# Turning the attention weights by 32x32 blocks and DMAs instead of matrix transposes, in a four-layer graph kernel

## The reference, cut to what matters

```python
Wh = jnp.einsum('bnf,fo->bno', h, W)
s1, s2 = Wh @ a1, Wh @ a2
e = s1[:, :, None] + s2[:, None, :]
e = jnp.where(e >= 0, e, ALPHA * e)
e = jnp.where(adj_matrix[None] == 0, -jnp.inf, e)
attention = jax.nn.softmax(e, axis=-1)
h_prime = jnp.einsum('bij,bjo->bio', attention, Wh)
```

## Time and profile before

| | |
|---|---|
| time, median of 3 runs | 634.5 us (633.63 to 634.8) |
| time of the profiled execution | 635.21 us |
| its span, first to last instruction | 633.4 us |
| mean granted clock of PE | 0.996 of full speed |
| slots 3 to 6, each | 57.5 us |
| slots 2 and 7 | 57.3 and 57.6 us |

### The profile page before, as it was taken

The page is one execution under the profiler, slowest core; times in us unless marked ns, Lnnn a source line. Parts: engine busy times, 40 slices in busy tenths (PEclk is TensorE's granted clock), DMA queues, the critical chain, the costliest instruction groups (busy, mean ns, idle before and its releaser), DMA issues.

```text
span 633.4 us, 9530 instructions
## 1 busy us (share of the span) xinstructions
PE 617.9 (98%) x2738; PEld 433.9 (68%) x2738; DVE 470.4 (74%) x1623; ACT 435.6 (69%) x1000; POOL 167.3 (26%) x228
## 2 busy tenths in 40 slices
PE   9999999999999999999999999999999999999994
PEld 6645556448975686578568757865885686577794
DVE  3999999877847658866887787688769867365656
ACT  3678786957847765784777678567857766546774
POOL 1465541005332003204403240340143032103201
PEclk9999999999999999999999999999999999999998
DMA  8334000000000000000000000000000000000000
GB/s 331 136 130 167 1 2 0 0 1 2 1 1 1 1 2 0 2 1 34 2 1 1 33 2 1 35 2 1 1 33 2 0 35 1 1 0 35 1 35 35
DMA packets 4372, 16.85 MB, mean 27 GB/s; under 512 B 480, under 2 KB 480, under 8 KB 4192
## 3 DMA queue, kind: packets, MB, share of 16 engines
q1 hardware_dynamic: 4320, 16.25, 6.7%
HBM read 12.05 MB, written 4.19 MB: 26 GB/s over the span
## 4 chain that ended last, share of the span: by engine, by line
PE 77%; DVE 3%; ACT 3%; issue 2%; POOL 1%; ACTq 0%; POOLq 0%; DVEq 0%
PE QQ L855 26%; PE QQ L867 15%; PE PA L838 4%; PE PA L810 4%; PE PB L829 2%; PE PB L820 2%; PE PB L691 2%; PE PA L691 2%; PE PA L791 2%; PE PB L791 2%; PE PA L644 1%; PE QQ L889 1%; PE PB L908 1%; PE PB L770 1%; PE PA L770 1%
## 5 line engine op out<-in xcount | busy, mean ns | idle before, releaser
L1231 ACT ACTIVATE raw<-QQ,BL 128x256 f32<-128x256 f32 (+2 forms) x279 | 150.1, 558 | 75.1 <-PE QQ L867 37.7
L855 PE MATMUL QQ<-HT,WT 128*128 128x256 f32 (+2 forms) x558 | 183.9, 474 | 1.1 <-ACT raw L1231 0.6
L450 POOL TENSOR_TENSOR RSD<-VAR,pw 128x4 f32<-128x4 f32 (+1 forms) x43 | 61.8, 1438 | 376.2 <-DVE VAR L1454 376.2
L855 PEld LDWEIGHTS QQ<-HT,WT 128*128 128x128 f32 x558 | 103.5, 190 | 59.3 <-issue 28.3
L867 PE MATMUL QQ<-HB,WT 128*128 128x256 f32 (+2 forms) x336 | 100.2, 441 | 0.4 <-DVE HB L1740 0.2
L867 PEld LDWEIGHTS QQ<-HB,WT 128*128 128x128 f32 x336 | 61.2, 190 | 29.3 <-issue 13.4
L1267 ACT ACTIVATE raw<-raw 128x256 f32<-128x256 f32 (+4 forms) x79 | 37.1, 470 | 25.9 <-DVE raw L1722 19.7
L1712 DVE SCALAR_TENSOR_TENSOR raw<-raw 128x256 f32<-128x256 f32 (+2 forms) x60 | 32.5, 542 | 20.2 <-ACT raw L1231 19.6
L1740 DVE SCALAR_TENSOR_TENSOR HB<-raw 128x256 f32<-128x256 f32 (+4 forms) x42 | 20.1, 478 | 23.5 <-ACT raw L1267 23.5
L1066 ACT ACTIVATE X<-Z,OFF,RSD 128x128 f32<-128x128 f32 x80 | 31.8, 481 | 2.5 <-POOL OFF L456 2.5
L518 POOL TENSOR_SCALAR X<-four,MEAN,RSD 128x128 f32<-128x128 f32 x64 | 30.7, 494 | 1.6
(11 more groups left out here) (254 smaller groups left out, 1164.5 us busy)
## 6 DMA issues: line engine op xcount, KB each, us to landing
four<-in_x SPq DMA_DIRECT2D x8, 512.0 KB, 4.0
raw<-in_xt SPq DMA_DIRECT2D x8, 512.0 KB, 6.6
out<-four SPq DMA_DIRECT2D x7, 512.0 KB, 2.7
WT<-in_lstm SPq DMA_DIRECT2D x1, 2048.0 KB, 9.3
later<-in_later SPq DMA_DIRECT2D x1, 725.5 KB, 10.2
AD<-in_adj SPq DMA_DIRECT2D x2, 256.0 KB, 4.8
out<-four SPq DMA_DIRECT2D x2, 256.0 KB, 2.0
early<-in_early SPq DMA_DIRECT2D x1, 289.0 KB, 4.7
```

Source lines behind the costliest of these rows:

```text
L450: pool.tensor_tensor(RSD[kk][:, ts], VAR[kk][:, ts], pw[:, ts], ALU.pow).then_inc(ln[k]["rstd"], some)
L855: mm = pe.matmul(steps_view(Q[q], k), WT[:, 0, (p - 1) * 4 + q, :], ht_view(par, k), start=True, stop=(s == 0))
L1231: act.activation(TG[q][:, at:n], Q[q][:, at:n], ACT.Tanh, scale=0.5 if q == G else 0.25, bias=BL[:, p - 1, q:q + 1]).then_inc(g_ok, 1)
```

## The change

The 16 transposes on PE and the four copies on DVE go away in slots 2 to 7 (groups 0 and 1, ahead of the slots, keep theirs). In their place:

- DVE's `a_turn_blocks` does one block transpose for each batch: it turns every 32x32 block of `E1` within its 32 partitions and writes it into `MS`. It cannot bring a block to another quarter of the partitions.
- SP's `move_blocks` does that: for each half of the group (two batches) 16 DMAs, each of 32 partitions by 1 KB, from `MS` back to where `E1` was. So there are 32 DMAs in a slot. The first 16 wait until two batches are turned, the next 16 until four are, and the output of group `s - 3` stands behind them in the queue.
- PE's `a_mix` reads the weights in runs of 32 elements out of the moved blocks, and waits for all 16 DMAs of its half (`moved_ok`).
- The products stand in two pairs: batches 0 and 1 after `x(9)`, batches 2 and 3 after `x(10)`, with the projection of batch 0 ahead of `h(9)` and that of batch 1 after `x(10)`.
- On ACT `a_exps` of batch 3 moves behind `state(7)`, and on DVE `a_hidden` moves from before `cell(7)` to behind it.

```diff
+        def by_block(k, h):
+
+            return late[:, k, h * COLS:(h + 1) * COLS].rearrange("p (q b c m i) -> p q b c m i", q=4, b=2, c=NC, m=NC)
...
-            for g in range(GROUPS - 1):
-                sp.wait_ge(ln[3]["out"], TILES * (g + 1))
-                sp.dma_start(out[g], OUT[:, g % 2]).then_inc(sent[g % 2], 16)
+            def move_blocks(g, h):
+
+                sp.wait_ge(tr_ok, GB * (g - 2) + 2 * (h + 1))
+                for q in range(4):
+                    for c in range(4):
+                        sp.dma_start(late[32 * c:32 * c + 32, 1, h * COLS + q * NODES:h * COLS + (q + 1) * NODES],
+                                     late[32 * q:32 * q + 32, 0, h * COLS + c * NODES:h * COLS + (c + 1) * NODES]).then_inc(moved_ok[h], 16)
+
+            for s in range(2, GROUPS + 2):
+                if s < GROUPS:
+                    for h in range(2):
+                        move_blocks(s, h)
+                if s >= 3:
+                    g = s - 3
+                    sp.wait_ge(ln[3]["out"], TILES * (g + 1))
+                    sp.dma_start(out[g], OUT[:, g % 2]).then_inc(sent[g % 2], 16)
...
                 for b in some:
-                    pe.wait_ge(pt_ok, GB * (g - 1) + b + 1)
+                    pe.wait_ge(moved_ok[b // 2], 256 * (g - 1))
+                    reach(pe, h1_ok if b % 2 else y1_ok, 2 * g)
                     for m in range(NC):
-                        mm = pe.matmul(f.AB[b][:, 0:NODES], turned(X2, m, b), f.MS[:, 2 * b + m, :],
+                        mm = pe.matmul(f.AB[b][:, 0:NODES].rearrange("p (c q i) -> p c q i", c=NC, q=4), turned(X2, m, b),
+                                       by_block(1, b // 2)[:, :, b % 2, :, m, :].rearrange("p q c i -> p c q i"),
                                        start=(m == 0), stop=(m == NC - 1))
...
                 x(8)
-                a_turn_e(s, range(GB)) if A else None
                 h(8)
                 x(9)
                 if A:
-                    a_mix(s, (0, 1, 2))
-                    a_project_mix(s, (0, 1))
+                    a_mix(s, (0, 1))
+                    a_project_mix(s, (0,))
                 h(9)
                 x(10)
                 if A:
-                    a_mix(s, (3,))
+                    a_project_mix(s, (1,))
+                    a_mix(s, (2, 3))
                     a_project_mix(s, (2,))
                 h(10)
...
                 gates(7)
+                state(7)
                 a_exps(s, (3,)) if A else None
-                state(7)
                 cell(8)
-                a_mixed(s, (0, 1, 2)) if A else None
-                cell(9)
-                a_mixed(s, (3,)) if A else None
+                a_mixed(s, (0, 1)) if A else None
+                gates(9)
+                state(9)
+                a_mixed(s, (2, 3)) if A else None
                 cell(10)
...
+            def a_turn_blocks(g, some):
+
+                for b in some:
+                    dve.wait_ge(exps_ok, GB * g + b + 1)
+                    dve.wait_ge(lin_ok, GB * g + 2 * (b // 2 + 1))
+                    dve.transpose(by_block(0, b // 2)[:, :, b % 2].rearrange("p q c m i -> p (c m) q i"),
+                                  E1[:, 2 * b:2 * b + 2].rearrange("p c (m q i) -> p (c m) q i", m=NC, q=4)).then_inc(tr_ok, 1)
...
-                cell(6)
-                a_hidden(s - 1, 1 - par) if B else None
+                inner(6)
+                a_turn_blocks(s, (0,)) if A else None
+                state(6)
+                a_hidden(s - 1, 1 - par) if B and not A else None
                 norm_small(3, 2, s - 3) if T and A else None
+                a_turn_blocks(s, (1, 2)) if A else None
                 cell(7)
                 norm_small(3, 2, s - 3) if T and not A else None
-                a_weights(s, (0, 1)) if A else None
+                if A:
+                    a_turn_blocks(s, (3,))
+                    a_hidden(s - 1, 1 - par)
                 cell(8)
                 if A:
-                    a_weights(s, (2, 3))
                     a_inverse(s)
                     a_sum2_mix(s, (0, 1))
                 cell(9)
```

More of the change, by code:

```diff
@@ L251, in build @@
                              "turned_ok"))
-        copied_ok = sem("copied_ok")
+        copied_ok, tr_ok = sem("copied_ok"), sem("tr_ok")
+        moved_ok = [sem(f"moved_ok{k}") for k in range(2)]
         f_half, cf_half, cell_half, tc_half = (sem(n) for n in ("f_half", "cf_half", "cell_half", "tc_half"))
@@ L1179, in a_lin @@
                     act.wait_ge(max_ok, TILES * g + 2 * b + 2)
-                    reach(act, et_ps, GB * before(g))
+                    reach(act, et_ps, GB * before(g)) if g <= 2 else act.wait_ge(px_ps, GB * (g - 2))
                     for c in range(NC):
```

## The result

The changed kernel takes 688.45 us (median of four runs, 688.04 to 690.93), the kernel before 634.37 beside it: a ratio of 1.086, 95% interval 1.083 to 1.089. That is slower, as forecast, but by 54 us where 12 were forecast, and outside the range.

What follows compares the result with a forecast made beforehand. PE's own work bounds the six touched slots: waits of 2.37 and 1.43 less 1.74 us of transposes add 2.05 a slot, 1.68 in slot 2; 11.9 on 634.5 makes 646.4 us, range 634 to 657.

Steps and rivals of the forecast that it cites:

- rival 2: DVE's block transpose takes two passes, 1.36 us; 8.2 us more in all, 654.6 us; chance 0.03.
- the first issue: SP's first block DMA in slot 4 starts at 339.14, when batch 1's turn ends.
- the two waits for SP's queue: PE idles ahead of both pairs of products until their blocks land: 2.4 and 1.4 us a slot, 23 us in all.
- rival 3: Issues of 32 partitions are much cheaper, so blocks are there when PE comes: 4.0 us faster, 630.5 us; chance 0.15.
- The queue: SP issues 32 block DMAs in turn, 0.47 us apart; halves land at 347.5 and 355.0 in slot 4.
- the landing: Time from issue to arrival of a 32 KB block DMA: taken as 1.4 us, from above 2.0.
- the first wait: PE, ahead of the first pair of products, waits 2.4 us a slot for the first half to land.
- My bounds for the spacing: Time between SP's block DMA issues: at 0.42 us, the issue's own length, the kernel takes 640.5 us.
- Rival 4: PE's clock falls in its new gaps; matmuls between the waits at half speed cost 4.6 us a slot, 674; chance 0.04.
- the second wait: PE, ahead of the second pair of products, waits 1.4 us a slot for the second half to land.
- One more wait, hidden so far: DVE's row sums ahead of `cell(9)` make PE wait 1.08 us at `h(10)` if blocks come in time.

Runs made afterwards that it cites:

- the probe: The kernel before, with bursts of needless extra DMAs of several shapes and sources behind its seven outputs, into an unused buffer; 633.7 us.
- the divided run: The changed kernel with its 32 block DMAs a slot divided between SP and GpSimd as issuing engines; 638.77 us, ratio 1.008 to the kernel before.
- a better version: Changed kernel with blocks moved by way of HBM, batch 1's row sums behind the ninth cell, norm statistics behind batch 1's block transpose; 628.63 us, ratio 0.992.

## Why the prediction was wrong

**The direction and the mechanism held.** The 16 transposes went off PE without a gap, the block transposes took 0.71 us (0.68 taken, and not the 1.36 of rival 2), the first issue stood in its place (339.14), and the two waits for SP's queue took the place of the transposes. The kernel without DMAs came out at 631.3, where rival 3 has 630.5 for blocks that are there in time.

**The step that failed is "The queue": "Bytes make no difference there, so I take 0.47 for 32 partitions too".** The spacing was 0.633. I generalised over the two attributes that the rows varied or that I thought of, bytes and partitions, and neither made a difference in the probe; the third, that all rows of before had one end in HBM, I did not see. Up to the 16th issue this makes 2.5 us, and the landing, 1.8 in place of 1.4, adds 0.4: the last landing of the first half comes 2.9 us later than forecast, and the first wait is 5.07 us on the mean and not 2.4. From landing to landing it makes 16 x 0.633 = 10.13 in place of 7.5. My bounds for the spacing went from 0.38 to 0.47 only, though the row did not show the operation: the range had no end above for it, and that is why the time lies outside.

**Sum of the miss.** The six slots grew by 54.5 us, the forecast was 11.9, a miss of 42.6. First waits: 30.4 us in all against 13.9, 16.5. From the first pair to the second: 64.0 against 45.1, 18.9, of which 15.7 is the spacing and the rest single long issues, up to 1.6 us. The low clock behind the second landing: 3 x 1.7 = 5.1. That leaves 2.1 us, 0.35 a slot. The rows have nearly all of it: the wait counts from the end of `x(9)`, 1.89 us after its start, where the forecast went on after 1.73 (0.16); from `h(8)` to `x(9)` it is 1.83 and not 1.73 (0.10); and from the second pair to the end of the slot 4.42 and not 4.34 (0.08).

**Rival 4 (0.04) was no rival but a companion.** The clock did fall, in every slot, to 0.50. As the forecast said, its price is only what the second wait does not cover; as the queue was slower than forecast, that wait covered all but the 5.1 us of the second fall, which came in three slots. Its chance was too low: the one row of an idle PE showed 0.55.

**Rival 3** decided at a spacing of 0.35 and was far off. The rule of the Trainium skill ("DMA: Bandwidth & Descriptors", section "Issuing engines are not separate DMA queues") that the time to start a DMA is usually small relative to the DMA does not hold here: 0.59 us of issue to a landing of 1.8, and in a row of 32 the issues are 20 us of 22. What the same section says ahead of it, that issuing from several engines saves just this time, is what the divided run shows.

**"One more wait, hidden so far"** was right in its cause, the row sums, and in size (1.08 worked out, 1.05 measured once the DMAs were gone, 1.16 a slot gained when the sums were moved), but not in its place: PE stood at the projection of batch 2, for a copy of ACT behind `state(9)`, and not at `h(10)`. That the size came so near by another path is partly luck. It was where most of the gain of a better version lay.

## What to carry to other kernels

Before a step is traded for many small DMAs, multiply their number by the issue time of the very kind of DMA, with its two ends where they will be; where no row shows that kind, the bound above must be wide. An in-order queue was a threshold here: up to the time at which the consumer came it cost next to nothing, beyond it every issue cost, so fewer, larger transfers by a longer way can win. And a wait that covers a second cost hides it: measure with one of them taken out before adding both.

## What the runs showed of the hardware

- In a row of like ones, an issue by SP from on-chip to on-chip takes 0.59 us (0.63 apart), with 32, 64 and 128 partitions and rows of 1 and 4 KB; one with an end in HBM takes 0.33 to 0.44 us (0.46 to 0.48 apart). A DMA to HBM directly behind the on-chip ones took 0.58 us, alone 0.33. GpSimd issues the same on-chip DMA in 0.498 us; in the one kernel that had it do so the program's end came 5 us later.
- Single issues of 1.0 to 2.0 us stand in most runs, in kernels with the same order on SP at different places. Their cause stays open.
- TensorE's granted clock fell from 1.00 to 0.50 (its lower level, 1.2 GHz) within an idle time of 5 us in each of six slots of the changed kernel, and stayed at 1.00 with idle times of up to 1.8 us in the same places (constants in the waits).
